# Wide attention with the output weights multiplied into the values once per batch

## What is computed

```python
q = (query @ Wq + bq).reshape(b, sq, N_HEAD, KEY_DIM)          # 16 heads of 64
k = (key @ Wk + bk).reshape(b, key.shape[1], N_HEAD, KEY_DIM)
v = (value @ Wv + bv).reshape(b, value.shape[1], N_HEAD, VALUE_DIM)
scores = jnp.einsum('bqhd,bkhd->bhqk', q, k) / TEMP
attn = jax.nn.softmax(scores, axis=-1)
out = jnp.einsum('bhqk,bkhd->bqhd', attn, v).reshape(b, sq, N_HEAD * VALUE_DIM)
out = out @ Wo + bo + residual
return (out - mu) * jax.lax.rsqrt(var + EPS) * ln_gamma + ln_beta
```

## Time and profile before

| | us |
|---|---|
| median of 3 runs | 1577.11 |
| lowest and highest | 1574.54 and 1578.02 |
| span of the profiled execution | 1592.2 |
| of it the wide attention, about | 287 to 603 |
| PE busy in the span | 1297.0 (81%) |
| DVE, ACT, POOL busy | 946.5, 723.1, 527.5 |

### The profile page before, as it was taken

The page is one execution under the profiler, slowest core; times in us unless marked ns, Lnnn a source line. Parts: engine busy times, 40 slices in busy tenths (PEclk is TensorE's granted clock), DMA queues, the critical chain, the costliest instruction groups (busy, mean ns, idle before and its releaser), DMA issues. The chain is left out here.

```text
span 1592.2 us, 25277 instructions
## 1 busy us (share of the span) xinstructions
PE 1297.0 (81%) x8946; PEld 752.5 (47%) x8946; DVE 946.5 (59%) x2139; ACT 723.1 (45%) x1940; POOL 527.5 (33%) x625
## 2 busy tenths in 40 slices
PE   2799629579989977784997698989887977996998
PEld 2444317345656645463442455656554434442443
DVE  6466621444555655255664688888764875555664
ACT  3354413166656533342543465655755333454222
POOL 2320340525333361333100365656643320000444
PEclk8599859799999997895998799999988996998999
DMA  2444120330000002322000000000000001000000
GB/s 65 127 130 128 40 66 26 72 75 14 1 1 2 1 27 62 89 58 50 9 10 2 1 1 1 1 2 1 1 1 1 1 10 23 10 3 1 7 7 14
DMA packets 66991, 45.30 MB, mean 28 GB/s; under 512 B 17564, under 2 KB 60261, under 8 KB 66869
## 3 DMA queue, kind: packets, MB, share of 16 engines
q1 hardware_dynamic: 61013, 34.48, 8.4%
q0 software_dynamic: 4096, 8.40, 1.9%
q10 hardware_dynamic: 1760, 0.82, 0.3%
HBM read 24.91 MB, written 13.89 MB: 24 GB/s over the span
## 5 line engine op out<-in xcount | busy, mean ns | idle before, releaser
L3411 ACT ACTIVATE L2a_pr<-psum,L2a_negmax 128x512 f32<-128x512 f32 (+3 forms) x256 | 132.6, 532 | 94.0 <-DVE L2a_negmax L3537 40.1
L557 ACT ACTIVATE L1x_praw<-psum,L1x_negmax 128x154 f32<-128x154 f32 x256 | 96.5, 392 | 78.4 <-DVE L1x_negmax L649 78.2
L318 POOL TENSOR_TENSOR L1x_pm<-L1x_praw,L1x_total 128x1024 f32<-128x1024 f32 x32 | 60.7, 1898 | 160.6 <-DVE L1x_total L655 111.7
L3276 PE MATMUL psum<-ident,L2a_pr 128*128 128x128 f32 x640 | 85.9, 278 | 19.0 <-DVE L2a_pT L3550 11.7
L649 DVE TENSOR_REDUCE L1x_negmax<-psum 128x4 f32<-128x616 f32 x64 | 50.7, 794 | 55.2 <-PE psum L370 51.0
L3276 PEld LDWEIGHTS psum<-ident,L2a_pr 128*128 128x128 f32 x640 | 71.7, 143 | 24.7 <-issue 21.1
L1978 POOL TENSOR_TENSOR L3f_scaled<-L3f_sg,L3f_wide 128x512 f32<-128x512 f32 (+1 forms) x44 | 55.7, 1271 | 66.9 <-ACT L3f_sg L2057 37.9
L1611 DVE TENSOR_REDUCE L3x_negmax<-psum 128x6 f32<-128x924 f32 (+1 forms) x48 | 47.7, 1011 | 46.8 <-PE psum L1149 37.4
L1611 DVE TENSOR_REDUCE L0x_negmax<-psum 128x6 f32<-128x924 f32 (+1 forms) x48 | 47.8, 1010 | 44.9 <-PE psum L1149 40.6
L3161 POOL TENSOR_TENSOR L2a_pr<-L2a_pr,L2a_total 128x1024 f32<-128x1024 f32 x29 | 56.5, 1947 | 46.5 <-DVE L2a_total L3566 46.3
L3164 POOL TENSOR_TENSOR L2a_pr<-L2a_pr,L2a_total 128x768 f32<-128x768 f32 x32 | 48.7, 1520 | 70.0 <-DVE L2a_total L3566 69.7
(11 more groups left out here) (741 smaller groups left out, 3372.1 us busy)
## 6 DMA issues: line engine op xcount, KB each, us to landing
expert_arena<-in_L_ffn_w SPq DMA_DIRECT2D x16, 256.0 KB, 4.4
group_in<-zero SPq DMA_DIRECT2D x2, 1472.0 KB, 9.3
L1f_xs<-group_in SPq DMA_DIRECT2D x10, 256.0 KB, 3.8
group_out<-L1f_ys SPq DMA_DIRECT2D x10, 256.0 KB, 3.6
L1f_gu<-in_L_ffn_gate_up_w SPq DMA_DIRECT2D x8, 256.0 KB, 3.5
slots_in<-zero SPq DMA_DIRECT2D x1, 1280.0 KB, 9.0
L0f_xs<-slots_in SPq DMA_DIRECT2D x5, 256.0 KB, 3.6
resid<-in_x SPq DMA_DIRECT2D x4, 256.0 KB, 5.8
```

What stands on the lines that cost most here:

```text
L318: nc.gpsimd.tensor_tensor(pm[:, n % 2].rearrange("p j t k -> p (j t) k"), praw[:, n % 3, :, :, 0:MAIN].rearrange("p j t k -> p (j t) k"), ...
L557: nc.scalar.activation(praw[:, n % 3, j, t, :], psum[:, 2 * u + j, x * CTX:(x + 1) * CTX], ACT.Exp, bias=negmax[:, n % 2, u, j, x:x + 1], ...
L3276: last = nc.tensor.transpose(psum[:, TURN + n // 4, n % 4 * P:(n % 4 + 1) * P], pr[:, m % RING, n * P:(n + 1) * P], core.ident[:])
L3411: ins = nc.scalar.activation(pr[:, i % RING, SEQ * j + lo:SEQ * j + hi], psum[:, bank + j, lo:hi], ACT.Exp, bias=negmax[:, i % RING, e:e + ...
```

## The change

For each head the change multiplies the batch's values with that head's part of the output weights ahead of the units: `vw` holds, for 128 keys and each head, 128 numbers of output, and `vwt` the same for the tails of two units (four heads of 32 rows). A unit's products are then one matmul per head and query tile straight into bank OUT, and in odd units one per query tile for the tails of two units. The copy `oT` on ACT and the output matmuls are gone. To make the weight products, PE makes turned values (`values_turned`, three calls per batch, copied by ACT into `vT`, which lies in `core.x1`) and multiplies them with the output weights (`values_out`, four calls per batch, banks H0 and H1, copied by DVE in three pieces).

The products of unit m come in step m + 3 and the loop has 3 steps behind the last unit. The turned rows and the queries have a bank of their own (`IN`, number 6). Keys move to H0. `finished` has four parts at g = 3, 3, 5 and 6 of the next batch, part 0 between the two maxima. The fetches of batch 3 come at units 4 to 7 and their sum at unit 10.

```diff
-                    if n == 6:
+                    if n == 4:
                         pool.wait_ge(s["summed"], 3)
-                    if 6 <= n < 10:
-                        fetch(3, 2 * (n - 6), 2 * (n - 5))
+                    if 4 <= n < 8:
+                        fetch(3, 2 * (n - 4), 2 * (n - 3))
...
+                def values_turned(b, i, bank):
+
+                    g0, g1 = key_unit(i)
+                    for g in range(g0, g1):
+                        last = nc.tensor.matmul(psum[:, bank, (g - g0) * KP:(g - g0 + 1) * KP], w["wv"][:, g * P:(g + 1) * P], core.ctxp[:, b, :],
+                                                start=True, stop=True)
+                    last.then_inc(s["vt_ps"], 1)
+
+                def values_out(b, i, bank):
+
+                    pe.wait_ge(s["vt"], 3 * b + (2 * i + 1) // 3 + 1)
+                    for part in (0, 1):
+                        for x in range(2):
+                            g = 2 * i + x
+                            for j in range(G):
+                                rows, k = slice(DK * j, DK * j + DK), 2 * j + x
+                                wo = w["wo"][rows, g * P:(g + 1) * P]
+                                if part == 0:
+                                    last = nc.tensor.matmul(psum[:, bank + j, x * D:(x + 1) * D], vT[rows, g, 0:MAIN], wo, start=True, stop=True)
+                                else:
+                                    last = nc.tensor.matmul(psum[32 * k:32 * k + 32, bank + j, 2 * D:3 * D], vT[rows, g, MAIN:KP], wo, start=True, stop=True)
+                    last.then_inc(s["vw_ps"], 1)
...
                     pe.wait_ge(s["pt"], 2 * m + 2)
-                    pe.wait_ge(s["tt"], m // 2 + 1)
...
-                        nc.tensor.matmul(psum[DK * j:DK * j + DK, OV, :], vm[:, b % 2, h * DK:(h + 1) * DK], pT[:, m % 3, j, :], start=True, stop=True)
-                    nc.tensor.matmul(psum[:, OV, :], vt[:, b % 2, g * P:(g + 1) * P], tT[:], start=False, stop=True, skip_group_check=True).then_inc(s["pv"], 1)
...
+                    pe.wait_ge(s["vw"], 4 * b + g // 2 + 1)
                     if g == 0 and b:
                         pe.wait_ge(s["yr"], b)
-                    for t in range(QT):
-                        last = nc.tensor.matmul(psum[:, OUT, t * P:(t + 1) * P], oT[:, m % 2, t * P:(t + 1) * P], w["wo"][:, g * P:(g + 1) * P],
-                                                start=(g == 0 and t == 0), stop=False, skip_group_check=True)
+                    for j in range(G):
+                        for t in range(QT):
+                            last = nc.tensor.matmul(psum[:, OUT, t * P:(t + 1) * P], pT[:, m % 3, j, t * P:(t + 1) * P], vw[:, b % 2, g, j, :],
+                                                    start=(g == 0 and t == 0 and j == 0), stop=False, skip_group_check=True)
+                    if g % 2:
+                        pe.wait_ge(s["tt"], m // 2 + 1)
+                        for t in range(QT):
+                            last = nc.tensor.matmul(psum[:, OUT, t * P:(t + 1) * P], tT[:, t * P:(t + 1) * P], vwt[:, b % 2, g // 2, :],
+                                                    start=False, stop=False, skip_group_check=True)
...
                         if m >= 2:
                             pe.wait_ge(s["tt"], m // 2)
+                        if follows and g in (3, 6):
+                            pe.wait_ge(s["k"], 3 * (b + 1) + (1 if g == 3 else 2))
+                        if n < NS and b and g == 0:
+                            pe.wait_ge(s["k"], 3 * (b + 1))
+                        if follows and g in (3, 4, 6):
+                            pe.wait_ge(s["vt"], 3 * (b + 1) + (3, 4, 6).index(g) + 1)
+                        if follows and g in (5, 7):
+                            pe.wait_ge(s["vw"], 4 * (b + 1) + (5, 7).index(g) + 1)
+                        if n < NS and b and g in (1, 2):
+                            pe.wait_ge(s["vw"], 4 * b + 2 + g)
...
-                    if 0 <= n - 4 < NS:
-                        values(n - 4)
...
+                    if 0 <= n - 3 < NS:
+                        values(n - 3)
+                    if n < NS and follows:
+                        pe.wait_ge(s["q"], n + NG)
+                        if g == 0:
+                            rowsT(b + 1, IN)
+                        query(n + NG, IN)
...
+                        if follows and g in (2, 5, 7):
+                            keys(b + 1, (2, 5, 7).index(g), H0)
+                        if n >= 3 and n % 2 and (follows and g in (3, 5) or b and g == 1):
+                            pe.wait_ge(s["tt"], (n - 1) // 2)
+                        if follows and g in (2, 3, 5):
+                            values_turned(b + 1, (2, 3, 5).index(g), H1)
+                        if follows and g in (4, 6):
+                            values_out(b + 1, g // 2 - 2, H0)
+                        if b and g in (0, 1):
+                            values_out(b, 2 + g, H0)
-                    if 0 <= n - 5 < NS:
-                        output(n - 5)
...
-                def value(b, i, bank):
-                    dve.wait_ge(s["v_ps"], 4 * b + i + 1)
+                def values_out(b, i, bank):
+                    dve.wait_ge(s["vw_ps"], 4 * b + i + 1)
...
+                    nc.vector.tensor_copy(vw[:, b % 2, 2 * i:2 * i + 2].rearrange("p x j d -> p j x d"),
+                                          psum[:, bank:bank + 2, 0:2 * D].rearrange("p j (x d) -> p j x d", d=D))
+                    for j in range(G):
+                        rows = slice(2 * 32 * j, 2 * 32 * j + 64)
+                        ins = nc.vector.tensor_copy(vwt[rows, b % 2, i, :], psum[rows, bank + j, 2 * D:3 * D])
+                    ins.then_inc(s["vw"], 1)
...
                     if 0 <= n - 2 < NS:
                         turned(n - 2)
+                    if b and b < B and g == 3:
+                        finished(b - 1, 0)
                     if n < NS:
                         maxima(n, 1)
...
+                        if g == 3:
+                            finished(b - 1, 1)
+                        if g == 5:
+                            finished(b - 1, 2)
+                        if g == 6:
+                            finished(b - 1, 3)
```

More of the change, by code:

```diff
@@ L425, in _ @@
                     keys(0, i, i)
-                for i in range(4):
-                    value(0, i, 3 + i)
+                for i in range(3):
+                    values_turned(0, i, 3 + i)
                 for g in range(NG):
@@ L430, in _ @@
                 last.then_inc(s["bo_ps"], 1)
[L431 to L436, removed]
+                pe.wait_ge(s["k"], 3)
+                values_out(0, 0, 0)
+                values_out(0, 1, 2)
+                pe.wait_ge(s["vt"], 3)
+                values_out(0, 2, 4)
+                pe.wait_ge(s["vw"], 1)
+                values_out(0, 3, 0)
                 pe.wait_ge(s["bo"], 1)
@@ L558, in exps, with values_turned @@
                                                  bias=negmax[:, n % 2, u, j, x:x + 1], accum_out=total[:, n % 2, j, t:t + 1]).then_inc(s["ex"], 1)
-                def values(m):
-                    act.wait_ge(s["pv"], m + 1)
-                    if m >= 2:
-                        act.wait_ge(s["op"], m - 1)
-                    nc.scalar.activation(oT[:, m % 2, :], psum[:, OV, :], ACT.Copy).then_inc(s["o"], 1)
+                def values_turned(b, i, bank):
+                    g0, g1 = key_unit(i)
+                    act.wait_ge(s["vt_ps"], 3 * b + i + 1)
+                    if i == 0 and b:
+                        act.wait_ge(s["vw_ps"], 4 * b)
+                    nc.scalar.activation(vT[:, g0:g1, :].rearrange("p g k -> p (g k)"), psum[:, bank, 0:(g1 - g0) * KP], ACT.Copy).then_inc(s["vt"], 1)
                 def root(b):
@@ L577, in _ @@
                 rows_root(1)
-                for n in range(NS + 5):
+                for n in range(NS):
                     b, g = n // NG, n % NG
@@ L582, in _ @@
                         grouped.spread_root(act, 0)
-                    if n < NS:
-                        exps(n, 0)
-                        exps(n, 1)
-                    if 0 <= n - 4 < NS:
-                        values(n - 4)
-                    if n < NS and b + 1 < B:
+                    exps(n, 0)
+                    exps(n, 1)
+                    if b + 1 < B:
                         if g == 0:
-                            rowsT(b + 1, H0)
-                        query(n + NG, H0)
+                            rowsT(b + 1, IN)
+                        query(n + NG, IN)
                         if g in (2, 5, 7):
-                            keys(b + 1, (2, 5, 7).index(g), H1)
+                            keys(b + 1, (2, 5, 7).index(g), H0)
+                        if g in (2, 3, 5):
+                            values_turned(b + 1, (2, 3, 5).index(g), H1)
                     if b == B - 1 and g == 2:
@@ L705, in _ @@
                 normed(1)
```

(9 more changed lines are left out.)

135 lines of the change are left out of this document (37 added, 98 removed).

## The result

The change made the kernel slower: 1583.34 us median of 4 runs against 1575.82 for the kernel before, ratio 1.0053 (95% interval 1.0036 to 1.0070), 7.5 us. Six more runs beside other runs of the kernel before gave 1586.15 against 1576.64, ratio 1.0052 (1.0034 to 1.0071). The forecast was "within 0.2%", 1576.6 us; the time lies in the range of 1567 to 1587, the sign was missed.

The account below looks back on a forecast made before the run. PE's issue order was taken to bound the stage; unit 27 about 5 us later, then two fewer units at the end swallowed by POOL, middle -0.5 us: 1577.11 - 0.5, rounded to 1576.6 us, range 1567 to 1587.

Parts of the forecast that it names:

- the end of the stage: After unit 27: POOL ends at about 597.8, stage at 600 (598 to 602) against 603.0 or 598.7.
- the +5 of unit 27: Unit 27 starts +3.7 to +5.9 us later, taken as +5, on 531.18 us.
- the scatter lands 1 to 4 us later: Stage end: the last scatter lands 1 to 4 us after POOL ends at about 597.8.
- The signs that I had named as right: Products 1.9 and 2.8 us, 0.6 us waits, unit 27 about 5 us later, last scatter after 592.77, last product before 590.
- Start: Start of the stage: first rows summed earlier, as DVE has fewer evictions; 1.1 to 3.3 us gained.
- the 2.4 of units 2 to 4: Some 2.4 us of waits in units 2 to 4 are filled by products that start a unit earlier.
- rival 3: New products: weight loads don't overlap, 640 passes at 0.11 us more, some 70 us, 1647 us; chance 0.01.
- (a): Next unit's transposes wait for DVE's eviction of each weight product: 0.62 us, 12 times, 7.4 us.
- (b): Waits for ACT's eviction of keys and turned values: 0.2 to 0.5 us at 9 places, 3.2 us.
- I keep 35.6 us: Last units: unit 30's weights are scaled 35.6 us after unit 27's start, as before, bounds 3 us.
- Rival 2: Last batch: DVE becomes the bound through moved finishing and (a) waits of 1.0 us; 10 us later, 1587 us; chance 0.28.
- Rival 1: Faster: clock stays up in units 27 to 29, cheaper weight products, evictions half hidden; about 8 us, 1569 us; chance 0.34.

Follow-up runs that it names:

- the second profile of the old order: Profile of the kernel before with only the last eight fetches moved, from units 6 to 9 to units 4 to 7: 1576.52 us, ratio 1.0000.
- edits of 8 and 6 us: Changed kernel with the sum read ahead of the turned-weight copies (1575.02 us), or batch 2's finishing put back (1576.97 us); both together 1575.91 us.
- the sum first: Changed kernel with DVE reading the finished batch's sum ahead of the two copies of turned weights: 1575.02 us, ratio 0.9995 to the kernel before.
- one bank: Changed kernel with weight products made in 24 calls in the queries' bank, between scores and products: 1567.50 us, ratio 0.9935 to the kernel before.

## Why the prediction was wrong

**The step that failed most is the end of the stage.** My -0.5 us had three parts: -2.0 and +7.0 make the +5 of unit 27, and -5.5 is what is left for the end. Against the second profile of the old order they came out so, the last one up to the first instruction of the next stage:

| part | forecast | measured |
|---|---|---|
| start of the stage to the first scores | -2.0 | -0.6 |
| first scores to unit 27 | +7.0 | +9.2 |
| unit 27 to the end | -5.5 | +0.2 |
| stage | -0.5 | +8.8 |

The 5.5 us are 63.8 us for the change (35.6, 26.0 and 2.2) against 71.9 or 67.5 for the old order, near the middle of the two. The 71.9 hold the delay in front of the last sum, which the plain runs don't have: 1.8 of the 5.5 us were this delay and no gain. That "the scatter lands 1 to 4 us later" was 2.2 us in the sum; the next stage began 4.94 us behind the last scatter, 2.7 us more. POOL ended 62.7 us after unit 27's start, where I had 61.6, 1.1 us more. That POOL would end the stage was right, but with these sizes the old order, which DVE ended, was no slower there.

My new end of 600, 313.0 us after the stage's start, lies near the 311.3 at which DVE ended, but by luck: it holds the 4.9 us by which the start was late in the execution that I read, and the changed kernel's execution did not have them.

The signs that I had named as right came: the passes, waits of 0.6 us behind each weight product, a last scatter after 592.77 (it ended at 596.65) and a last product before 590. Unit 27 came later too, though by 2.8 us instead of about 5 on the profile's time; counted from the stage's start it was 8.7 us later than in the second profile. None of these signs tests the number that is subtracted.

**Start.** Forecast 1.1 to 3.3 us earlier; measured 0.6 (33.93 to 33.37). I had the first sum 3.5 us earlier than the 305.35 of the earlier trace rows, which is 18.35 us after the stage's start. The old order without the delays has it 14.45 us after the start, the changed kernel 15.05, where I had 14.8. So the sum does not come earlier at all; the 3.9 us belonged to the execution. The first sum of the old order with the fetches moved (start of the stage 283.97), then of the changed kernel (286.04):

```profile
298.42 1.25 DVE L613 TENSOR_TENSOR L1x_praw<-L1x_praw,slot_wt 128x1024 f32<-128x1024 f32 x1
```

```profile
301.09 1.23 DVE L614 TENSOR_TENSOR L1x_praw<-L1x_praw,slot_wt 128x1024 f32<-128x1024 f32 x1
```

**The loop to unit 27.** Forecast +7.0 without the start, measured +9.2. From all of PE's records in the two stretches (from the start of one group to the start of the next, less idle):

| term | forecast | measured |
|---|---|---|
| products of units | -10.9 | -10.0 |
| value matmuls | -7.4 | -7.0 |
| turned values, 9 calls | +7.5 | +7.9 |
| weight products, 12 calls | +13.8 | +12.0 |
| other PE work | 0 | +2.4 |
| waits ahead of transposes | +8.2 | +10.1 |
| waits for the tails' copy | -4.6 | -4.4 |
| turned rows, queries | -2.1 | -3.2 |
| wait for the sum | +2.5 | +2.0 |
| small waits | 0 | -0.7 |

(The forecast of the sixth line is 7.4 and 3.2 less the 2.4 of units 2 to 4.) The first two lines rest on passes 0.11 us apart, and the timeline of the changed kernel has them so: 16 passes in 1.89 us, 24 in 2.78, one weight product in 0.99 to the next scores, which wait for nothing, and the transposes behind them 0.63 us:

```profile
429.89 2.05 PE L419 MATMUL psum<-L1x_vw,L1x_pT 128*128 128x128 f32 x16
431.78 1.06 PE L424 MATMUL psum<-L1x_vwt,L1x_tT 128*128 128x128 f32 x8
432.67 1.02 PE L345 MATMUL psum<-L1x_xnT,projections 128*128 128x512 f32 x2
433.63 0.71 PE L372 MATMUL psum<-projections,x 64*128 64x128 f32 x8
434.27 0.42 PE L374 MATMUL psum<-projections,x 64*32 64x128 f32 x8
434.62 0.79 PE L388 MATMUL psum<-L1x_kT,L1x_qT 64*128 64x154 f32 x8
436.05 1.07 PE L399 MATMUL psum<-ident,L1x_pm 128*128 128x128 f32 x8 [0.63 <-issue]
```

So rival 3 is out, and the sentence of the Trainium skill, "TensorE: Matmul & The Clock Gate", Part 3, that I weighed is not what these passes show. Of the waits, (a) was right: twelve of 0.63 us. Of (b), 3.2 us at nine places, one of 1.7 us came. What the forecast lacked are the two waits of 1.55 us in units 16 and 24, where DVE came late for the maxima, of which I had said that "they have a unit's slack", and 1.6 us of half clock in unit 18, which is in the fifth line.

**The last units.** "I keep 35.6 us, and bounds of 3 us": the weights of unit 30 were scaled 37.0 us after unit 27's start, and POOL's own work took 25.7 us for 26.0. The number nearly held, but it hid what was to be had: with the finishing of batch 2 put back the same place is at 28.8 us, and POOL ends 55.1 us after unit 27's start instead of the old order's 61.1. So the finishing that moved into units 29 and 30, which I put at nothing within 3 us, cost 7.6 us up to the next stage and 6.4 in the plain runs. I named the table of experts behind the finishing, and did not price the ranks, which stand between DVE and the bank of PE's transposes.

**Rival 2** had the place right, DVE in the finishing steps when PE needs it, and a time of 1587. Its mechanism was another: the waits of (a) stayed at 0.63 us instead of rising to 1.0, and the adding step that took 2.54 us in the earlier trace rows took 0.74, though POOL was scaling for 0.59 us of it (566.63 to 567.76):

```profile
566.48 0.74 DVE L759 SCALAR_TENSOR_TENSOR L1x_y<-L1x_y,gate,resid 128x512 f32<-128x512 f32 x1
...
566.63 1.13 POOL L324 TENSOR_TENSOR L1x_pt<-L1x_praw,L1x_total 128x104 f32<-128x104 f32 x2
```

The rule of the Trainium skill that I had weighed, "SBUF — State Buffer", "Who interferes with whom", is not what this step shows; DVE's order decided. **Rival 1** put the clock on the faster side; it came on the slower.

## What to carry to other kernels

Before a forecast is subtracted from a profiled time, find where the profile exceeds the plain runs: idle time with no releaser may belong to the execution, and the old stage has to be priced without it. A stage ends where the next one begins: ask which engine releases that, before and after. An eviction that stands in the order of the engine that sets the time costs more than its wait: what is queued behind the copy comes late too, and the clock can fall; another bank and place gave 15 us in the stage where the waits behind the copies were 7.6. Finishing work goes behind, not ahead of, the small reads that release a bank.

## What the hardware showed beside this

In the changed kernel a tensor engine that stood for 1.6 and 3.1 us in units 28 and 30 went on at half clock (1.2 GHz), and the fall came or stayed away with edits elsewhere, so that edits of 8 and 6 us gave 7 together. It also reached into the next stage, whose code is the same in all versions. In every trace a stretch of half clock lies over the border. From the next stage's first instruction to the first matmul of the next attention the lengths were 103.9 to 104.2 us in the five traces where that stretch lasted 17.1 us (among them the sum first and one bank), 106.9 and 108.0 in the two with 20.5 us, and 106.6 to 109.5 in the seven with 23.9 us (among them the kernel before and the changed kernel). So versions differ by up to 5.6 us behind the stage that the change touches. That the length of that stage follows from the clock is read from these traces and was not tried by itself.
